# Graph attention with a residual layer norm: where the last graph's attention stands, two buffers of split attention, and the order of flags, residuals and loads

## The reference

```python
scale = HIDDEN ** -0.5
q = (x @ Wq.T).reshape(b, n, 12, 32)
k = (x @ Wk.T).reshape(b, n, 12, 32)
v = (x @ Wv.T + bv).reshape(b, n, 12, 32)
scores = einsum('bqhd,bkhd->bhqk', q, k) * scale + (adj + adj)[:, None]
row_nonzero = any(scores != 0, axis=-1, keepdims=True)
scores = where(row_nonzero, scores, -inf)
p = nan_to_num(softmax(scores, axis=-1))
out = einsum('bhqk,bkhd->bqhd', p, v).reshape(b, n, 384) @ Wo.T + bo
x = _layernorm(x + out)          # eps 1e-5, no gain or shift
```

## Time and profile before

| | us |
|---|---|
| median of 3 runs | 622.47 |
| lowest, highest | 622.44, 625.47 |
| profiled execution, its own time | 624.42 |
| span of its instructions | 622.6 |
| PE busy | 608.4 (98%) |
| ACT busy | 503.1 (81%) |
| DVE busy | 474.1 (76%) |
| POOL busy | 409.8 (66%) |

### The profile page before, as it was taken

One profiled execution on the slowest core, in us unless ns is written; L12 is line 12 of the kernel. 1 busy time (PEld: TensorE's weight loads), 2 busy tenths in 40 slices (PEclk: granted clock), 3 DMA queues, 4 the chain that ended last, 5 costly groups with the idle time before them and its releaser, 6 DMA issues.

```text
span 622.6 us, 22866 instructions
## 1 busy us (share of the span) xinstructions
PE 608.4 (98%) x8248; PEld 505.4 (81%) x8248; DVE 474.1 (76%) x2374; ACT 503.1 (81%) x1946; POOL 409.8 (66%) x500
## 2 busy tenths in 40 slices
PE   9999999999999999999999999999999999999985
PEld 5788888888888888888888888888888888887764
DVE  4677877877877787787787787787787788778882
ACT  5788878878887887988878887887888888787971
POOL 1675766767767666766767676676776766765661
PEclk9999999999999999999999999999999999999996
DMA  8411324222142322224232132323214222212111
GB/s 299 150 38 33 123 88 133 82 100 95 50 137 89 127 86 73 85 85 139 84 132 87 30 127 87 131 86 114 72 58 137 90 76 88 62 46 81 53 53 51
DMA packets 33424, 58.51 MB, mean 94 GB/s; under 512 B 9888, under 2 KB 22688, under 8 KB 33312
## 3 DMA queue, kind: packets, MB, share of 16 engines
q1 hardware_dynamic: 32880, 56.47, 27.3%
q10 hardware_dynamic: 432, 0.59, 0.3%
HBM read 43.52 MB, written 13.53 MB: 92 GB/s over the span
## 4 chain that ended last, share of the span: by engine, by line
PE 92%; DVE 4%; issue 1%; POOL 1%; DMA 1%; ACT 0%; SPq 0%; POOLq 0%; DVEq 0%; ACTq 0%
PE qk_ps L338 34%; PE vo_ps L370 15%; PE vo_ps L424 15%; PE scores_ps L355 8%; PE scores_ps L382 8%; PE att_ps L404 8%; PE qk_ps L424 2%; PE scores_ps L436 1%; DVE nscores L567 1%; DMA nscores<-wk 1%; POOL tree L289 1%; DVE stats L647 0%; DVE y L644 0%; DVE att_t L635 0%; PE vo_ps L436 0%
## 5 line engine op out<-in xcount | busy, mean ns | idle before, releaser
L475 ACT ACTIVATE probs<-nscores,neg_max 128x128 f32<-128x128 f32 x768 | 298.0, 394 | 88.3 <-DVE neg_max L567 88.3
L567 DVE CUSTOM_DVE_ANT_0 nscores<-scores_ps,adj_n 128x128 f32<-128x128 f32 x768 | 167.3, 287 | 23.6 <-PE scores_ps L355 23.6
L475 ACT ACTIVATION_READ_ACCUMULATOR probs<-nscores,neg_max 128x1 f32 x768 | 147.3, 192 | 0.0
L289 POOL TENSOR_TENSOR tree<-nscores 128x768 f32<-128x768 f32 x64 | 120.4, 1881 | 17.6 <-DVE neg_max L567 17.6
L271 POOL TENSOR_TENSOR x_t<-x_raw,x_t 128x512 fp32r<-128x512 f32 x45 | 59.0, 1313 | 80.6 <-ACT x_t L492 80.6
L370 PE MATMUL vo_ps<-w_v,x_t 128*128 128x384 f32 x576 | 111.8, 338 | 0.0
L338 PE MATMUL qk_ps<-x_t,w_q 128*128 128x512 f32 x405 | 110.5, 411 | 0.0
L289 POOL TENSOR_TENSOR tree<-tree 128x384 f32<-128x384 f32 (+1 forms) x128 | 103.9, 811 | 10.0
L338 PE MATMUL qk_ps<-x_t,w_k 128*128 128x512 f32 x405 | 110.4, 410 | 0.0
L370 PEld LDWEIGHTS vo_ps<-w_v,x_t 128*128 128x128 f32 x576 | 102.3, 188 | 6.1
L424 PE MATMUL vo_ps<-w_o,att_t 128*128 128x384 f32 x522 | 101.4, 338 | 0.0
(11 more groups left out here) (62 smaller groups left out, 682.8 us busy)
## 6 DMA issues: line engine op xcount, KB each, us to landing
x_n<-xn SPq DMA_DIRECT2D x32, 384.0 KB, 4.0
out<-out_n SPq DMA_DIRECT2D x31, 384.0 KB, 3.1
x_raw<-xt SPq DMA_DIRECT2D x15, 768.0 KB, 6.4
scale_t<-scale_mem SPq DMA_DIRECT2D x58, 192.0 KB
adj_n<-adj SPq DMA_DIRECT2D x32, 128.0 KB, 4.0
scale_mem<-scale_rows SPq DMA_DIRECT2D x58, 16.0 KB
x_raw<-xt SPq DMA_DIRECT2D x3, 256.0 KB, 5.0
nscores<-wq ACTq DMA_DIRECT2D x3, 192.0 KB, 4.1
```

The costliest lines, as they stand in the source:

```text
L289: nc.gpsimd.tensor_tensor(tree[:, b % 2, :, 0:width], src[:, :, 0:width], src[:, :, width:2 * width], ALU.add).then_inc(tree_step, 1)
L475: last = nc.scalar.activation(probs[:, b % 2, h], nscores[:, b % 2, h], ACT.Exp, bias=neg_max[:, b % 2, h:h + 1], scale=-1.0, accum_out=ro ...
L567: last = nc.vector.tensor_tensor_reduce(out=nscores[:, half, h], in0=scores_ps[j][:, m * P:(m + 1) * P], in1=adj_n[:, b // 2 % 2, half], s ...
```

## The change

Nine edits. (1) `att_t` gets two buffers, chosen by `b % 2`, and `attention_high(b)` waits for `project_out(b-2)` only. (2) The attention of the last graph, with its `total` and `nonzero`, is written to `vo_ps` (`att_bank`), and so no longer waits for `att_ps`. (3) In `turn`, the flag `probs_ready` is waited for by thirds, ahead of each four heads. (4) Behind the last `turn` stands one more matmul on zeros. (5) `find_scale` takes the reciprocal behind the two instructions on the tree's sums, with one more wait. (6) POOL sums the scores ahead of adding bo. (7) SP asks for x of the next pair ahead of the store of the last one, when `y` of the pair that held the buffer is made. (8) `residual(61)` moves behind the copy of the turned probabilities in step 63, and ACT normalises 61 and 62 in step 64; bank 2 of graph 62 is copied by DVE, not by ACT. (9) The last graph is normalised by DVE as (y - mean) * rstd, from `rstd` alone; POOL makes no `shift` for it.

```diff
+        def att_bank(b):
+            return att_ps if has(b + 1) else vo_ps
         def low_banks(b):
-            return 3 if ending(b) and b < NB - 1 else 2
+            return 3 if ending(b) and b < NB - 2 else 2
# SP
                     if pair >= 1:
+                        if pair + 1 < NB // 2:
+                            sp.wait_ge(y_ready, b - 1)
+                            sp.dma_start(x_n[:, (pair + 1) % 2], xn[pair + 1]).then_inc(xn_in[(pair + 1) % 2], DMA)
                         sp.wait_ge(out_ready, b - 1)
                         sp.dma_start(out[pair - 1], out_n[:, (pair - 1) % 2]).then_inc(stored[(pair - 1) % 2], DMA)
-                        if pair + 1 < NB // 2:
-                            sp.dma_start(x_n[:, (pair + 1) % 2], xn[pair + 1]).then_inc(xn_in[(pair + 1) % 2], DMA)
-                sp.wait_ge(out_ready, NB - 1 + half)
+                sp.wait_ge((out_ready, last_ready)[half], (NB - 1, 1)[half])
# POOL, find_rstd
                                         ALU.pow).then_inc(rstd_ready, 1)
+                if not has(b + 1):
+                    return
                 pool.wait_ge(rstd_ready, b + 1)
# POOL, loop
+                if has(b + 1):
+                    sum_scores(b + 1)
                 if has(b):
                     add_bias(b)
-                if has(b + 1):
-                    sum_scores(b + 1)
# PE, turn
-                pe.wait_ge(probs_ready, KT * (b + 1))
                 pe.wait_ge(biased, KT * (min(b + 1, NB - 1) + 1))
                 for h in range(HEADS):
+                    if h % HPT == 0:
+                        pe.wait_ge(probs_ready, KT * b + h // HPT + 1)
# PE, attend
-                wait(pe, att_split, b)
+                if has(b + 1):
+                    wait(pe, att_split, b)
-                        last = nc.tensor.matmul(att_ps[j * D:(j + 1) * D, m * P:(m + 1) * P],
+                        last = nc.tensor.matmul(att_bank(b)[j * D:(j + 1) * D, m * P:(m + 1) * P],
# PE, loop
                 if b == NB - 1:
+                    run_idle(1, out_bank(b - 1))
                     attend(b)
                     project_out(b - 1)
# ACT
-                wait(act, oproj_done, b)
+                wait(act, oproj_done, b - 1)
-                if has(b - 2):
+                if b == NB:
+                    normalised(b - 3)
+                if has(b - 2) and b != NB - 1 and has(b - 1):
                     normalised(b - 2)
# DVE, find_scale
-                dve.wait_ge(probs_ready, KT * (b + 1))
-                wait(dve, recip_done, b)
-                nc.vector.reciprocal(recip[:], row_sum[:, half]).then_inc(recip_done, 1)
...
+                    if has(b + 1):
+                        dve.wait_ge(att_high, b)
...
+                dve.wait_ge(probs_ready, KT * (b + 1))
+                wait(dve, recip_done, b)
+                nc.vector.reciprocal(recip[:], row_sum[:, half]).then_inc(recip_done, 1)
                 dve.wait_ge(nonzero_done, b + 1)
+                dve.wait_ge(recip_done, b + 1)
# DVE, the last result
+            def normalised_last(b):
+                half = b % 2
+                dve.wait_ge(rstd_ready, b + 1)
+                dve.wait_ge(stored[b // 2 % 2], b // 4 * DMA)
+                nc.vector.tensor_scalar(out_n[:, b // 2 % 2, half], y[:, half], mean_var[:, half, 0:1],
+                                        rstd[:, half:half + 1], ALU.subtract, ALU.mult).then_inc(last_ready, 1)
# DVE, loop
                     if has(b):
                         keep_turned_high(b)
+                    if b == NB - 1:
+                        residual(b - 2)
...
                 if b == NB:
                     residual(b - 2)
-                if has(b - 1) and b != NB - 1:
+                if has(b - 1) and b < NB - 2 or b == NB:
                     residual(b - 1)
+            normalised_last(NB - 1)
```

More of the change, by code:

```diff
@@ L73, in build @@
         scale_n = sb("scale_n", [P, 2, HID])
-        att_t = sb("att_t", [P, 2, KT, P], F32R)
+        att_t = sb("att_t", [P, 2, 2, KT, P], F32R)
         y = sb("y", [P, 2, HID])
@@ L93, in build @@
         att_ps = ps("att_ps", [P, 512])
-        total = att_ps[:, HID:HID + HEADS]
-        nonzero = att_ps[:, HID + HEADS:HID + 2 * HEADS]
         scale_mem = nc.dram_tensor("scale_mem", (2, D, P), F32, kind="Internal").ap()
@@ L152, in build @@
         out_ready = sem("out_ready")
+        last_ready = sem("last_ready")
         def has(b):
@@ L423, in project_out @@
                     for n, (a, c) in enumerate(TERMS):
-                        last = nc.tensor.matmul(out_bank(b)[:, 0:HID], att_t[:, a, k], w_o[:, c, k],
+                        last = nc.tensor.matmul(out_bank(b)[:, 0:HID], att_t[:, b % 2, a, k], w_o[:, c, k],
                                                 start=(k == 0 and n == 0),
@@ L501, in attention_high @@
                 act.wait_ge(att_done, b + 1)
-                wait(act, oproj_done, b)
-                nc.scalar.activation(att_t[:, HI].rearrange("p m q -> p (m q)"), att_ps[:, 0:HID],
+                wait(act, oproj_done, b - 1)
+                nc.scalar.activation(att_t[:, b % 2, HI].rearrange("p m q -> p (m q)"), att_bank(b)[:, 0:HID],
                                      ACT.Copy).then_inc(att_high, 1)
@@ L586, in find_scale @@
                 half = b % 2
-                dve.wait_ge(probs_ready, KT * (b + 1))
-                wait(dve, recip_done, b)
-                nc.vector.reciprocal(recip[:], row_sum[:, half]).then_inc(recip_done, 1)
+                total = att_bank(b)[:, HID:HID + HEADS]
+                nonzero = att_bank(b)[:, HID + HEADS:HID + 2 * HEADS]
                 dve.wait_ge(tree_step, TREE * (b + 1))
                 if direct(b - 1):
-                    dve.wait_ge(att_high, b)
+                    if has(b + 1):
+                        dve.wait_ge(att_high, b)
                 else:
@@ L630, in normalise @@
                     scale = scale_t[:, b % 2]
-                nc.vector.tensor_tensor(att_ps[:, 0:HID], att_ps[:, 0:HID], scale, ALU.mult).then_inc(att_done, 1)
+                nc.vector.tensor_tensor(att_bank(b)[:, 0:HID], att_bank(b)[:, 0:HID], scale, ALU.mult).then_inc(att_done, 1)
             def attention_low(b):
                 dve.wait_ge(att_high, b + 1)
-                nc.vector.tensor_tensor(att_t[:, LO].rearrange("p m q -> p (m q)"), att_ps[:, 0:HID],
-                                        att_t[:, HI].rearrange("p m q -> p (m q)").bitcast(F32),
+                nc.vector.tensor_tensor(att_t[:, b % 2, LO].rearrange("p m q -> p (m q)"), att_bank(b)[:, 0:HID],
+                                        att_t[:, b % 2, HI].rearrange("p m q -> p (m q)").bitcast(F32),
                                         ALU.subtract).then_inc(att_split, 1)
```

## The result

The changed kernel takes 619.91 us (median of 13 runs, 619.36 to 623.98), the kernel before 622.90 us in the same set (13 runs, 622.31 to 627.21). The ratio is 0.995 with a 95% interval of 0.993 to 0.9969: faster by 0.5%, 3.0 us, where 6.2 us and 616.3 us were forecast. The time lies above the range. The profiled execution took 619.91 us of its own, with a span of 617.7 us.

What follows compares the result with a forecast made beforehand. PE was taken to bound the kernel from 21 to 565 us, with waits between engines and half clock at the end. Terms of -5.83, -0.49 and +0.1 gave -6.2 us: 622.47 becomes 616.3, range 615.3 to 619.4.

Steps and rivals of the forecast that it cites:

- the sum: Whole kernel: -5.83 - 0.49 + 0.1 = -6.2 us, taken from the median of 622.47 us to give 616.3.
- The 5.83 us: End of the kernel: the last output projection ends at 611.01 us in place of 616.84, 5.83 us sooner.
- Factors (edit 5): `find_scale` to `scale_n` on DVE: 0.72 us in step 63, against 0.68 before; 0.1 us cost over the five steps before.
- Clock: PE's end: one gap of about 0.3 us replaces 1.37 and 1.38, so full clock holds to the end.
- the clock falls all the same: Rival, 10%: the clock gate closes at 607.1 us as before, both last projections take 3.2 us each, total 619.1.
- Sum of scores (edits 6, 7): POOL, graph 63: x lands by 590.6 us, so the last tree is done at 601.95, not 604.66.
- DVE of step 63 (edit 8): DVE near the end: `normalise(62)` directly follows `attend(62)`, gaining 0.5 us; the second bank's copy, about 0.66 us, is covered.
- Turn (edits 3, 4): Last turn on PE: factors' transposes 1.4 us sooner, `attend(63)` at 606.26; the added matmul's 1.1 us hidden by copies.
- Last graph (edits 1, 2): Between the last two projections: a gap of 0.25 us in place of 1.22; the last starts at 609.15 us.
- Result (edit 9): Behind the last rstd: wait 0.39 to about 0.04 us, instruction 0.71 to 0.57 us, together 0.49 us sooner.
- PE's stream in the other graphs: Two added waits in each `turn`, 128 in all: cost 0, with 6.5 us as the dear bound.

Runs made afterwards that it cites:

- before, again: The kernel before, unchanged, run and profiled once more: 622.57 us (median of 12 runs), ratio 0.9994 to the kernel before; profiled execution 622.52 us, span 620.7.

## Why the prediction was wrong

**The step that failed is the sum**: "the median of the runs, 622.47, becomes 616.3". It subtracts a saving read in one profiled execution from the median of others. The 5.83 us were right for the two profiles (16.87 to 11.03 us, 5.84), but 1.9 us of them were clock that fell in that execution over more work than in the common ones, which have 14.97 us there. The prediction itself had noted that this execution took 624.42 us against a median of 622.47, and had carried the difference of 1.95 us as if it lay outside the end. The rest of the miss is one mis-sized term, one that was missing, and some chance. From the profile of the common kind of before to that of the changed kernel the spans go:

| stretch | before, again | changed | forecast change | measured |
|---|---|---|---|---|
| to the first score | 20.51 | 21.14 | 0 | +0.63 |
| first score to `project_out(57)` | 547.60 | 547.92 | 0 | +0.32 |
| four steps to `project_out(61)` | 31.86 | 32.47 | +0.1 | +0.61 |
| to the end of the last projection | 14.97 | 11.03 | -5.83 | -3.94 |
| to the end of the span | 5.76 | 5.14 | -0.49 | -0.62 |
| around the span | 1.8 | 2.2 | 0 | +0.4 |

The sum is -2.6 us between these two profiled executions; the medians differ by 3.0. The miss of 619.9 - 616.3 = 3.6 us is then 1.9 of clock, 1.2 beyond the forecast 0.1 in body, steps and around the span, and 0.6 ahead of the first score, less 0.1 at the result.

- *Factors (edit 5)*, forecast 0.1 us with bounds of 0 to 0.5: the edit costs 0.6 us in the steps, 0.3 in the body and 0.4 around the span, and undoing it gives 1.7 us at the medians, 1.4 between the fastest. Mis-sized: the order, which costs 0.8 us in the profiles; it is 0.78 us to `scale_n` and not 0.72, since the durations came from the other order and a reduce alone grew from 0.30 to 0.36. Missing: the added wait was taken as satisfied and so nearly free; the prediction asked of PE's waits whether they stand alone, and not of this one, which stands alone 57 times and moves the borders of DVE's list.
- *Clock*: right for the changed kernel as far as its profile goes (1.00 to the last projection). The rival "the clock falls all the same" came true in part of the executions: four of the 13 have a span of 618.6 to 618.9 at 0.995, and one 621.8 at 0.993; where in them it fell isn't recorded. And the assumption behind the sum, that before always pays for 9.9 us of half clock, was wrong.
- *Sum of scores (edits 6, 7)*: right. Edit 7 alone does it; edit 6 alone wasn't run. Undoing both costs 1.5 us at the medians.
- *DVE of step 63 (edit 8)*: right in kind; the net is 0.28 us.
- *Turn (edits 3, 4)*: right; the waits inside cost nothing (547.91 and 547.92 us for the body, 22,924 instructions with and without them), the added matmul is hidden behind the copies.
- *Last graph (edits 1, 2)*: right, 0.20 us between the projections where 0.25 was walked; but they also earn 0.64 us at the factors, which the walk put down to other edits.
- *Result (edit 9)*: right, 0.6 us measured alone where 0.49 was forecast.
- *PE's stream in the other graphs*: 547.92 against 547.60 us is a shift, but not by a constant for each graph and not from the waits in turn; two pauses of DVE made it.
- *To the first score* the profiles range from 20.47 to 21.59 us with the same code there, by when the load of Wo lands (9.6 us after its issue in the first profile of before, 10.2 in the changed kernel's, 10.8 in the slowest start). The 0.63 is taken as chance.

## What to carry to other kernels

Before a saving from a trace is subtracted, ask whether the profiled execution is typical: its own time against the median is the check, and where they differ by as much as the effect, the part that varies (here the clock) has to be taken out of the terms first. An end made of waits between engines is worth walking through edit by edit, which hit 11.03 us within 0.02. And in a group of small dependent instructions that sets the loop, leave the independent one first, and look whether a wait that an edit adds is an instruction of its own: even a satisfied one moves everything behind it in the engine's list.

## What the runs showed of the hardware that was not expected

- With the same waits, the clock in the last 15 us differed from execution to execution: attention and both projections at 1.2 GHz, or one projection, or (judged by the one span of 618.9 at 0.998) hardly any. Nine matmuls of the projection took 1.85 us at 2.4 GHz and 3.25 at 1.2 GHz.
- The reduce of 192 elements took 0.30 us behind the reciprocal and 0.36 us behind the accumulator read of the scores.
- DVE's queue stood 0.40 to 0.42 us ahead of the 2,880th instruction of its recorded list in all fourteen traces, with an 8 KB transfer of the instruction queue q14 0.65 to 1.0 us behind. Fifty-seven more satisfied waits moved that border from under a long instruction (0.18 us more for the step) to the front of `scale_n` (0.25 to 0.35), let two or three such pauses show in the body, and came with 0.4 us more around the span.
